# QKV products in native fp32 from an unsplit norm, with tiles normalised in groups of 6 and 12, and a new order of x products, turns and two pairs of layer two

## The reference

```
n   = (x - mean_c(x)) / sqrt(var_c(x) + 1e-6)              # norm over channels
qkv = w_qkv (288 x 96) @ n + b_qkv                          # per pixel
qkv = maxpool 2x2, then depthwise 3x3 convolution + bias    # 24 x 24 pixels
q, k normalised over the pixels; attn = q k^T * temperature # 8 heads of 12 channels
out = sum over 4 keep-counts of a_i * topk_softmax(attn) @ v
out = gelu(out), each pixel doubled both ways; x2 = x + w_proj @ out + b_proj
t   = norm over channels of x2 (1e-5)
probs = softmax(t @ gate_w + gate_b); the best 2 of 4 experts, renormalised
y   = x2 + sum_e p_e * (gelu(t @ w1_e + b1_e) @ w2_e + b2_e)   # 96 -> 384 -> 96
```

## Time and profile before

| | |
|---|---|
| Time, median of 3 runs | 152.74 us (151.22 to 153.0) |
| The profiled execution's own time | 153.1 us |
| Its span | 151.3 us |
| Mean granted TensorE clock, of full speed | 0.977 |
| Busy: TensorE products / weight loads | 138.7 / 114.9 us |
| Busy: VectorE / ScalarE / GpSimd | 113.7 / 80.5 / 59.6 us |

### The profile page before, as it was taken

How to read it: one execution, slowest core, us unless ns; L and a number is a source line. 1 busy time by engine, 2 the same in 40 slices (tenths; PEclk the granted TensorE clock), 3 DMA queues, 4 the chain that set the end, 5 groups by cost and what they waited for, 6 DMA issues and landing times.

```text
span 151.3 us, 2487 instructions
## 1 busy us (share of the span) xinstructions
PE 138.7 (92%) x778; PEld 114.9 (76%) x778; DVE 113.7 (75%) x317; ACT 80.5 (53%) x147; POOL 59.6 (39%) x60
## 2 busy tenths in 40 slices
PE   6946977999999899799999999999999999999990
PEld 2422866999969694667766689999999999999950
DVE  0799557999988379998502599998897899799713
ACT  3282759302253233656488456656766665676540
POOL 8999875860000000140602763324252332434250
PEclk9995599999999999999999999999999999999999
DMA  4589400000000000000000010010001001000101
GB/s 135 216 198 267 90 0 4 0 0 2 0 4 0 0 0 2 0 0 4 0 0 0 0 39 4 0 39 2 2 0 39 0 0 39 0 0 4 39 0 39
DMA packets 3750, 4.43 MB, mean 29 GB/s; under 512 B 1934, under 2 KB 3290, under 8 KB 3644
## 3 DMA queue, kind: packets, MB, share of 16 engines
q1 hardware_dynamic: 3338, 3.86, 10.2%
q10 hardware_dynamic: 402, 0.44, 0.8%
HBM read 3.42 MB, written 0.88 MB: 28 GB/s over the span
## 4 chain that ended last, share of the span: by engine, by line
PE 78%; DVE 11%; ACT 4%; DMA 4%; issue 1%; SPq 1%; DVEq 0%
PE psum L949 16%; PE psum L950 15%; PE psum L951 15%; PE psum L1119 9%; DMA xT<-xt 4%; PE psum L988 3%; PE psum L986 3%; PE psum L991 3%; PE psum L1044 3%; PE psum L1092 3%; PE psum L1029 3%; DVE xn_lo L644 2%; PE psum L944 2%; PE psum L922 2%; ACT xn_hi L473 1%; DVE stats L716 1%
## 5 line engine op out<-in xcount | busy, mean ns | idle before, releaser
L440 POOL TENSOR_TENSOR xs<-xs,yg 96x384 f32<-96x384 f32 x23 | 26.5, 1151 | 45.3 <-DVE yg L884 37.3
L657 DVE TENSOR_TENSOR h_lo<-hf,h_hi 128x768 fp32r<-128x768 f32 x25 | 34.4, 1378 | 5.1 <-ACT hf L550 4.6
L949 PE MATMUL psum<-xn_hi,w_hi 97*128 97x384 f32 (+1 forms) x72 | 28.7, 398 | 0.0
L950 PE MATMUL psum<-xn_hi,w_lo 97*128 97x384 f32 (+1 forms) x72 | 24.3, 337 | 0.0
L951 PE MATMUL psum<-xn_lo,w_hi 97*128 97x384 f32 (+1 forms) x72 | 24.2, 337 | 0.0
L550 ACT ACTIVATE hf<-psum 128x768 f32<-128x768 f32 x25 | 20.2, 809 | 5.7 <-PE psum L951 5.7
L433 POOL TENSOR_TENSOR xs<-xs,pr 96x384 f32<-96x384 f32 x6 | 5.1, 870 | 37.8 <-DVE gs L703 30.9
L949 PE MATMUL psum<-h_hi,w_hi 128*96 128x384 f32 x50 | 17.0, 339 | 0.0
L950 PE MATMUL psum<-h_hi,w_lo 128*96 128x384 f32 x50 | 16.8, 336 | 0.0
L951 PE MATMUL psum<-h_lo,w_hi 128*96 128x384 f32 x50 | 16.8, 336 | 0.0
L1119 PE MATMUL psum<-h_whole,w2s 128*96 128x384 f32 x44 | 16.1, 489 | 0.0
(11 more groups left out here) (173 smaller groups left out, 273.9 us busy)
## 6 DMA issues: line engine op xcount, KB each, us to landing
xs<-x SPq DMA_DIRECT2D x1, 864.0 KB, 9.9
out<-xs SPq DMA_DIRECT2D x6, 144.0 KB, 1.9
w1s<-w SPq DMA_DIRECT2D x1, 576.0 KB
w2s<-w SPq DMA_DIRECT2D x1, 576.0 KB, 6.7
xT<-xt SPq DMA_DIRECT2D x1, 432.0 KB, 5.3
xT<-xt SPq DMA_DIRECT2D x1, 288.0 KB, 3.7
pars<-par ACTq DMA_DIRECT2D x1, 196.5 KB
cst<-consts ACTq DMA_DIRECT2D x1, 170.0 KB, 5.3
```

What stands on the lines that cost most here:

```text
L440: pool.tensor_tensor(cols(xs, c), cols(xs, c), cols(yg, e), ALU.add).then_inc(acc_done, 1)
L657: dve.tensor_tensor(lo, h, hi.bitcast(F32), ALU.subtract).then_inc(h_split, 1)
L949: pe.matmul(o, w_hi, m_hi, start=start, stop=False)
L950: pe.matmul(o, w_lo, m_hi, start=False, stop=False)
```

## The change

- **QKV.** The turned chunk is copied by ScalarE unrounded into `go` (free until the gelu output), and each QKV product is one native fp32 product of `pars` and `go`. `par_hi`, `par_lo` and the six low halves of the first norm go; only the 27 columns of convolution weights are still split (`dw_hi`, `dw_lo`).
- **Order of QKV.** By pairs: k, q and v of chunks 0 and 1 first, then the rest. The turns stand ahead of the products (1,0), (1,2), (0,3) and (1,4), with no idle products of their own. The start has 27 idle products, not 24.
- **Norm.** Groups of 6 and 12 tiles, not 9 and 9. ScalarE normalises chunks 1, 3 and 5. The first pooling stands inside the second group's scale chain. The row of ones of `xn_hi` is set by VectorE at the start; GpSimd sets that of `go`.
- **ScalarE's order.** The nine `diag_hi` move behind the first two copies; `w1_hi` and `qd_hi` behind the last copy; `w2_hi` behind `qp_hi`. GpSimd's `w2_lo` moves behind `qp_lo`.
- **x products.** Three tiles ahead of the turns of k, three ahead of the scores, twelve behind them; the idle products at the first two places go, and there are two, not one, behind the last.
- **Layer two.** Turns 1 to 4 stand at pairs 3, 4, 5, 5 of chunk 0, not at 2, 3, 4, 5. Pairs (0, 5) and (1, 0) are no longer whole but split; VectorE splits (0, 5) behind the low half of chunk 4. ScalarE takes the high half of chunk 0 ahead of its copy of the first projection; one idle product goes.

```diff
-IDLE = {"start": 24, "convolved": 3, "before scores": 1, "softmax": 1, "turned": 2}
-IDLE_TURN = (0, 3, 3, 0, 0, 0)
-BY_SCALAR = (1, 4, 5)
+IDLE = {"start": 27, "softmax": 2, "turned": 1}
+BY_SCALAR = (1, 3, 5)
+FIRST = 6
-TURNS_IN_FIRST = ((), (), (1,), (2,), (3,), (4,))
-WHOLE = {0: (0, 1, 2, 3, 4, 5), 1: (0, 1, 2), NCH - 1: (4, 5)}
+TURNS_IN_FIRST = ((), (), (), (1,), (2,), (3, 4))
+WHOLE = {0: (0, 1, 2, 3, 4), 1: (1, 2), NCH - 1: (4, 5)}
+PREFILL = ((3, 4, 5), (6, 7, 8), (9, 10, 11, 12, 0, 1, 2, 13, 14, 15, 16, 17))
+PAIR_ORDER = ((1, 0), (0, 0), (2, 0), (1, 1), (0, 1), (1, 2), (0, 2), (2, 1), (2, 2))
+QKV_ORDER = tuple((g, 2 * h + i) for g, h in PAIR_ORDER for i in range(2))
+PAIR_BANK = {pair: (0, 2, 6)[i % 3] for i, pair in enumerate(PAIR_ORDER)}
+TURNS_AHEAD = {(1, 0): (0, 1), (1, 2): (2, 3), (0, 3): (4,), (1, 4): (5,)}
...
@@ GpSimd
+            pool.memset(go[C:C + 1, :], 1.0).then_inc(go_set, 1)
-            low(par_lo[:, :], pars[:, 0:P_SPLIT], par_hi[:, :], par_split)
+            low(dw_lo[:, :], pars[0:C, P_DW:P_DW + 27], dw_hi[:, :], dw_split)
...
@@ ScalarE, up to the convolutions
+            act.activation(dw_hi[:, :], pars[0:C, P_DW:P_DW + 27], ACT.Copy).then_inc(dw_split, 1)
+            def copy_turned(c):
+                act.wait_ge(ln[0]["turned"], c + 1)
+                act.activation(cols(go, c)[0:C], bank(turn_bank(0, c), cols=CH), ACT.Copy).then_inc(xn_copied, 1)
+            normalise(1)
+            copy_turned(0)
+            copy_turned(1)
+            # wx copied, the nine diag_hi
...
+            normalise(3)
+            copy_turned(2)
+            copy_turned(3)
+            normalise(5)
+            copy_turned(4)
+            copy_turned(5)
+            # w1_hi, qd_hi, kp_hi, qp_hi, w2_hi, ident_b
...
@@ VectorE, first norm
+                def beside_first(step):
+                    statistics(FIRST + step)
+                def beside_second(step):
+                    if step == 6:
+                        pool(1, 0)
+                for k in range(FIRST):
+                    statistics(k)
+                scale(slice(0, FIRST), beside_first)
+                for k in range(TPC):
+                    normalise(k)
+                for k in range(FIRST + 9, NT):
+                    statistics(k)
+                scale(slice(FIRST, NT), beside_second)
+                for c in (2, 4):
+                    for k in range(c * TPC, (c + 1) * TPC):
+                        normalise(k)
+            dve.memset(xn_hi[C:C + 1, :].bitcast(F32), 1.0).then_inc(lastrow_set, 1)
...
@@ TensorE
+            for i, (g, c) in enumerate(QKV_ORDER):
+                for d in TURNS_AHEAD.get((g, c), ()):
                     turn_back(0, d)
+                pe.wait_ge(xn_copied, c + 1)
...
+                if i % 2 == 0 and i >= 6:
+                    pe.wait_ge(pool_done, i // 2 - 2)
+                pe.matmul(bank(PAIR_BANK[g, c // 2] + c % 2, cols=CH), pars[:, w], cols(go, c),
+                          start=True, stop=True).then_inc(qkv_done, 1)
```

More of the change, by code:

```diff
@@ L123, in high_by_scalar, with pairs_until @@
 def high_by_scalar(c, p):
-    return p in HIGH_BY_SCALAR[1 if is_chunk(c, 1) else 2]
+    return not (is_chunk(c, 0) or is_chunk(c, 1)) and p in HIGH_BY_SCALAR
+def pairs_until(c, p):
+    return (divmod(n, NPAIR) for n in range(c * NPAIR + p + 1))
 def hi_count(c, p):
[L130 to L134, removed]
+    if isinstance(c, int):
+        return sum(not is_whole(d, q) and not high_by_scalar(d, q) for d, q in pairs_until(c, p))
+    each = NPAIR - len(HIGH_BY_SCALAR)
+    return (2 * NPAIR - EARLY_WHOLE) + (c - 2) * each + sum(not high_by_scalar(c, q) for q in range(p + 1))
 def splits(c, p):
-    return c * NPAIR + p + 1 - NPAIR - len(WHOLE[1])
+    if isinstance(c, int):
+        return sum(not is_whole(d, q) for d, q in pairs_until(c, p))
+    return c * NPAIR + p + 1 - EARLY_WHOLE
 def no_split_ahead(c, p):
@@ L416, in _ @@
             low(qp_lo[:, :], pooled[:, 0:PAD * PAD], qp_hi[:, :], qp_split)
+            pool.wait_ge(w_high, 2)
+            low(w2_lo[:, :], w2s[:, :], w2_hi[:, :], w_split)
             pool.memset(gateT[:, :].bitcast(F32), 0.0).then_inc(ones_set, 1)
@@ L732, in beside_first, with pool @@
                 def beside_first(step):
-                    statistics(9 + step)
+                    statistics(FIRST + step)
                 def beside_second(step):
[L736 to L741, removed]
+                    if step == 6:
+                        pool(1, 0)
+                for k in range(FIRST):
                     statistics(k)
-                scale(slice(0, 9), beside_first)
-                for k in range(3):
+                scale(slice(0, FIRST), beside_first)
+                for k in range(TPC):
                     normalise(k)
[L746 to L754, removed]
+                for k in range(FIRST + 9, NT):
[4 more added lines that the diff above has]
+                        normalise(k)
+            def pool(g, h):
                 dve.wait_ge(qkv_done, 1 + QKV_ORDER.index((g, 2 * h + 1)))
@@ L959, in _ @@
                       start=True, stop=True).then_inc(wx_mm, 1)
[L960 to L968, removed]
-                    turn_back(0, d)
[L970 to L973, removed]
+            pe.wait_ge(go_set, 1)
+            for i, (g, c) in enumerate(QKV_ORDER):
+                for d in TURNS_AHEAD.get((g, c), ()):
+                    turn_back(0, d)
+                pe.wait_ge(xn_copied, c + 1)
+                if i == 2:
+                    pe.wait_ge(wx_set, 1)
+                    pe.matmul(bank(7, C + 1, XW), pars[0:C, P_PW:P_PW + C + 1], cst[0:C, K_CEN:K_END],
+                              start=True, stop=True).then_inc(wx_mm, 1)
+                elif i == 5:
                     pe.wait_ge(wx_set, 2)
-                if c % 2 == 0 and pair in POOLED_BEFORE:
-                    pe.wait_ge(pool_done, 1 + POOL_ORDER.index(POOLED_BEFORE[pair]))
+                if i % 2 == 0 and i >= 6:
+                    pe.wait_ge(pool_done, i // 2 - 2)
                 w = slice(P_QKV + g * C, P_QKV + (g + 1) * C)
-                three(bank(PAIR_BANK[pair] + c % 2, cols=CH), par_hi[:, w], par_lo[:, w], cols(xn_hi, c),
-                      cols(xn_lo, c)).then_inc(qkv_done, 1)
+                pe.matmul(bank(PAIR_BANK[g, c // 2] + c % 2, cols=CH), pars[:, w], cols(go, c),
+                          start=True, stop=True).then_inc(qkv_done, 1)
             def conv(at, taps, w_hi, w_lo, p_hi, p_lo, split, done):
@@ L1010, in turn, with prefill @@
                 ins.then_inc(qkT_done, 1)
-            idle(IDLE["convolved"], 3)
+            def prefill(tiles):
+                for k in tiles:
+                    ins = pe.matmul(x2_tile(k, XW), xs[:, k * 128:(k + 1) * 128], cst[0:C, K_CEN:K_END],
+                                    start=k in (0, TPC, TPC + XP, TPC + 2 * XP), stop=False, skip_group_check=True)
+                return ins
+            pe.wait_ge(x_in, 16)
+            pe.wait_ge(wx_set, 2)
+            pe.wait_ge(k_ready, 2)
+            prefill(PREFILL[0])
             pe.wait_ge(khat_ready, 1)
@@ L1018, in _ @@
                 turn(0, b)
-            idle(IDLE["before scores"], 5)
+            prefill(PREFILL[1])
             pe.wait_ge(qkT_copied, 4)
@@ L1024, in _ @@
             ins.then_inc(score_done, 1)
-            pe.wait_ge(x_in, 16)
-            pe.wait_ge(wx_set, 2)
-            for k in range(NT):
-                ins = pe.matmul(x2_tile(k, XW), xs[:, k * 128:(k + 1) * 128], cst[0:C, K_CEN:K_END],
-                                start=k in (0, TPC, TPC + XP, TPC + 2 * XP), stop=False, skip_group_check=True)
-            ins.then_inc(x2_prefilled, 1)
+            prefill(PREFILL[2]).then_inc(x2_prefilled, 1)
             idle(IDLE["softmax"], 3)
```

116 lines of the change are left out of this document (50 added, 66 removed).

## The result

The changed kernel takes 163.21 us (median of 4, 162.62 to 164.66), the kernel before 152.07 in the same comparison: ratio 1.0745, 95% interval 1.063 to 1.086. It is 11 us slower where 7.5 faster were forecast. Medians are of all executions; a ratio is of those alone that lie within 1.5% of the fastest of their kernel. The profiled execution has a span of 160.8 us against 151.3, so 9.5 us have to be found.

The account below looks back on a forecast made before the run. TensorE, busy 92% of the span, was taken as the bound, with one clock dip and few idle stretches. Savings of 5.4 + 0.45 + 1.75 = 7.6 us gave 145.5, forecast 145.2 against the 152.74 median; range 143.6 to 148.4.

Parts of the forecast that it names:

- so the taps and the k norm shift along: After QKV: VectorE's last pooling ends 1.0 us after the last product (before 1.15), so the following steps move equally earlier.
- the gap at 15 to 17: QKV: after six products TensorE waits 1.85 us with only six turns, resuming at 16.75 after ScalarE's copy.
- Rival A: Clock falls in QKV's new gap: 2.0 us of gain gone, 147.2, up to 149 if it lasts; chance 0.22.
- a native product: QKV: an unsplit fp32 product takes 0.645 us against 0.53 split; 18 products go from 9.6 to 11.6 us.
- The term of 5.4 us: Start and QKV stage: the k convolution starts at 24.85 instead of 30.28, 5.4 us less.
- x products: Around k and the scores: with records moved, the attention matrix's turn starts at 50.35, before 50.8; 0.45 us less.
- Layer two: Layer two's reordered turns, split pairs, early high half and one idle product fewer save 1.75 us in sum.
- the wait at the gate turns: Layer two: TensorE reaches the gate turns at 73.85, VectorE's last low half comes at 74.45; turns end at 74.95.
- the two split pairs: Layer two: two pairs as split instead of native products cost 0.46 us less, their VectorE splits falling in idle time.
- Ahead of layer two: Taking the high half ahead of the projection and one idle product fewer give 0.2 us.
- B: Helpers late, kp_lo or the gate chain: 1 to 1.6 us lost, 146.5; chance 0.10 shared with a late ScalarE queue.
- C: Clock stays at 1.2 GHz over the whole QKV stage: slower by 2.1, 154.8; chance 0.03 including the unforeseen.

Follow-up runs that it names:

- e2_w2low_late: Changed kernel with GpSimd's w2_lo and the memsets behind it held back until the k norm is done; 160.87 us, ratio 1.057.
- e6_before_layer_two: Kernel before with only the four edits of layer two; 151.54 us, ratio 0.995.
- e3_clear_of_taps: Changed kernel with xn_lo's memset directly behind go's, w1_hi ahead of copy 4, w2_lo and later memsets held until attention is turned; 147.65 us, ratio 0.971.
- e8_memsets_early: e3_clear_of_taps with its two late GpSimd memsets (gateT, sel_b) moved from 49 to 16.2; 147.7 us, ratio 0.971.
- e4_before_w2low: Kernel before with only GpSimd's w2_lo moved behind qp_lo; 156.03, 156.99, 165.61 and 165.82 us in four executions, ratio 1.029 from two.

## Why the prediction was wrong

**The step that failed** is the one line "so the taps and the k norm shift along". It took the taps at their old price in a new neighbourhood. I had costed the new order of GpSimd by readiness alone, whether kp_lo comes when the convolution asks for it (it did, at 28.12, asked for at 28.73), and never asked what runs on VectorE meanwhile. In the old kernel GpSimd's low halves lay beside VectorE steps that read PSUM (poolings and low halves), and the taps beside memsets and a small cast. Shortening the stage and queueing w1_lo, kp_lo, qp_lo and w2_lo in one row put the taps 4.3 us into an unbroken 12 us of GpSimd work. The runs show 6.5 us for that (7.6 against 1.15). Against the old kernel, whose two taps took 1.6, the k chain also lost 6.5: 6.0 in the taps, 0.2 in the third step (1.04 for 0.80), and 0.3 by which the start of the convolution is recorded early (see the terms).

The Trainium skill ("SBUF — State Buffer", Who interferes with whom) states this: a VectorE copy or tensor_scalar in a two-port mode and a GpSimd instruction exclude one another for the whole instruction, and a VectorE instruction with two SBUF inputs is held only by a GpSimd one that reads SBUF. No trace names the mode of a step, but the traces agree in each form: tensor_scalar beside tensor_tensor (3.49 us for 0.58), tensor_scalar beside memset (2.12 for 0.32), two inputs beside w2_lo (2.60 for 0.45), and poolings out of PSUM unharmed (0.95 throughout). It was there to be read and would have given the rival that was missing.

**The clock** was a rival, in the wrong place. I weighed a fall only in the gap at 15 to 17 and over the QKV products, priced at 2 us; nowhere did I ask what a wait further on would do. TensorE stopped at 39.7 for 6 us, the clock was low for 27 us, and this is the larger part of the loss (8.6 of 15.1 us). Over the gap itself the clock held in the changed kernel (1.00 from 10 to 42, with 1.19 us idle and six turns in it). Rival A came true in `e2_w2low_late`, with 1.57 us idle there: the k convolution started near 27.5 (26.9 forecast for it).

**The terms.** Forecasts stand in brackets.

- First product at 10.95 (10.7), second scale at 14.07 (14.1), a native product 0.645 us (0.645; the poolings of pairs follow each other by 1.29).
- The gap ended at 17.51 (16.75), mostly since the tile beside GpSimd's memset came late; without that it ended at 17.00. So the k convolution started at 25.87 (24.85). The term of 5.4 us is 4.4 in the changed kernel, 4.9 with GpSimd clear (start at 25.36), and 5.5 with the diag_hi moved. Some 0.3 us of each belong to the records: the first k product is now recorded 0.43 us ahead of the second, where before it was 0.14, and the next stretch is longer by as much.
- x products: 0.49 us (0.45).
- Layer two: 1.2 us (1.75), and the wait at the gate turns came as said. In `e6_before_layer_two` the gate turns ended 15.4 us after the first product of layer two, before 16.45, which is the 1.1 summed for that. The term sized too large is that of the two split pairs: some 0.15 is left for it (0.46). Ahead of layer two 0.07 came (0.2).
- For `e3_clear_of_taps` the four stretches of the balance give 4.9 - 0.3 - 0.3 + 1.2 = 5.5 us of span, 151.3 to 145.8 (7.6). The first 0.3 is that of the records. The second is what GpSimd's memsets beside the second norm cost (0.8) less what the x products gave (0.5): `e8_memsets_early` passes that stretch in 15.6 us, `e3_clear_of_taps` in 16.5.

**The rivals.** B had the right suspects (GpSimd late) with the wrong harm: late results, not a held VectorE. C, the only slower one, put the clock over QKV. No rival had VectorE slowed by GpSimd, and 0.02 for slower was far too little for a change that reorders four queues.

## What to carry to other kernels

When work is moved on GpSimd, lay its new stretch over VectorE's timeline and read, step by step, what form VectorE has there: here steps that read PSUM kept their time, tensor_scalar steps out of SBUF did not, and a step with two SBUF inputs did not beside a GpSimd instruction that reads. A new wait of TensorE must be priced twice, once as a wait and once as the work behind it at 1.2 GHz (here 6 and 9 us). How short a wait is harmless these runs don't tell: the clock fell behind waits of 6, 2.1, and 1.1 and 1.6 us, and once behind two of about 0.6 and 0.4 that it withstood in another run. And when a large gain is sure in one stage, check each neighbour that the stage now slides over; here a 4.4 us gain and a new order on GpSimd slid the taps under a row of other work 12 us long.

## What was not expected of the hardware

- The clock, once down, stayed at 1.2 GHz from 43 to near 70 with TensorE busy 86% of the time, mostly on turns and products of about 100 columns; in the kernel before, where idle and QKV products followed from 13.94 on, it was back within 18 to 19.
- The executions of one program, `e4_before_w2low`, took 156.0 and 157.0, or 165.6 and 165.8 us, with a wait of 2.1 us in the traced one of the slower pair.
- A held step can lose to several GpSimd instructions in a row. In the changed kernel the first tap outlasts kp_lo and qp_lo (to 29.72) and ends at 30.85; the second ends at 34.89, behind w2_lo and the memset that ends at 34.38.
- VectorE's first tap alone takes 0.58 us; the 0.85 us of the kernel before, which the prediction carried along, stood beside the end of a memset (31.80).
- GpSimd suffers too: w2_lo took 3.69 us beside the taps, 2.69 before.
